# One piece of stacked operands issued earlier, and the order of five engines drawn up anew

## The chip, the cores and the metric

The kernel runs on one core of a Trainium2 chip. The metric is device microseconds (us) for one execution of the whole kernel. The time before is 529.72 us, the median of 3 runs (528.26 to 529.98). All durations below come from one profiled execution of the kernel before.

## The reference, cut to what matters

For each of 8 batches of 512 rows and 256 columns: layer norm, attention over 16 heads of 16 columns, layer norm and residual; then layer norm, a gated feed-forward layer, layer norm and residual.

```python
# x: (8, 512, 256); 16 heads of 16; weights are the same for all batches
x_proj = (layernorm(x) @ w_in.T + b_in).reshape(b, l, 16, -1)
q, k, v = split(x_proj, 3, axis=-1)
att = softmax(einsum('blhd,bmhd->blmh', q, k) * 0.25, axis=2)     # over m
opt = einsum('blmh,blhd->blhd', att, v)        # v of row l times the SUM of its softmax
x = x + layernorm(opt.reshape(b, l, 256) @ w_out.T + b_out)
top1 = argmax(softmax(layernorm(x) @ gate_W.T + gate_b))          # one of 8 experts
inter = relu(layernorm(x) @ wi_W.T + wi_b + lora_of(top1))        # 1024 columns
x = x + layernorm(inter @ wo_W.T + wo_b)
```

Because the attention sum runs over `m` while `v` is taken at `l`, the output of attention is `v` times a sum of softmax values that is 1 but for rounding. The kernel computes the sum from all scores all the same.

## The kernel before, in words

**Units.** A batch has 64 score units: 16 heads times 4 blocks of 128 query rows. For unit `i` TensorE (PE) makes one 128x512 matmul, the score (L227), VectorE (DVE) takes the negated maximum of each row (L692), and ScalarE (ACT) takes the exponential with its row sum (L505). The scores live in a ring of five PSUM banks `ps`, so the score of unit `i` waits until the exponential of unit `i-5` is done. Three more banks, `pu`, serve all other matmuls; a matmul group that takes a `pu` bank waits for the copy that empties it.

**Three engines, one order each.** The order of work on every engine is written out by hand as a table of calls. `slot(s)` in batch `b` is the score of unit `s+4` on PE, the maximum of unit `s+2` on DVE, and the exponential of unit `s` on ACT. Between the slots of batch `b` stand the parts of three neighbouring batches: the norm transposes `x_t(b+1)`, the projections `q_k(b+1, m)` and `value(b+1, t)` of the next batch; the attention output `o_t(b-1)`, `project(b-1)`, the gate and the first feed-forward matmuls `f1(b-1)` of the batch before; and `f2(b-2)` with its norm. Batches 2 to 6 run the same loop body. In batches 0 and 1 there is less of this work, and PE is filled with matmuls of ones that compute nothing (L206), one ahead of each score whose slot is not in the list `FULL`.

**From q_k to the scores.** A projection of 128 rows is evicted twice: ACT writes the rounded high part to `qk` (L519), DVE the low part (L706, semaphore `qk_low`). Then DMAs gather heads from `qk` into `stack`, the operand of the scores. A batch's heads come in four pieces, `stacks(b, 0)` to `stacks(b, 3)`, each 16 units, each 8 DMAs (L1141) issued by the sync engine's queue (SP). `stacks(b+1, 0)` waits for the last of the four low parts of batch `b+1`. `stack` holds three pieces in a ring. And `q_k(b+1, 0)` on ACT overwrites `qk`, so it first waits until the pieces of batch `b` have landed. I number pieces through all batches: batch 0 has pieces 0 to 3, batch 1 begins with piece 4.

**SP's order at the start.** Pieces 1 and 2, and between them `wi`, `lora`, `wib` (late inputs); then a wait for GpSimd (POOL) to have split `wo`, the inputs `x` of batches 2 and 3, which land where `wo` was staged, then piece 3.

**From the last exponential to the next steps.** When a batch's 64 sums are there, DVE computes `ratio` (L790) and `ratio_whole` (L795, `sone`), POOL scales `v` by it (`scale`, L1005), PE transposes it (`o_t`, L239), ACT copies it (L533), and PE projects it (`project`, L285).

Of the kernel before, what the change touches and what calls it, by code (L numbers as in the profile page):

```python
# [21 lines left out]
IDLE, FULL = (25, 6, 4), (8, 28, 32, 35, 39, 50, 53, 61, 69, 71, 73, 75, 76, 82, 84, 90, 96, 98, 99, 100, 102, 103,  # L22
                           105, 107, 109, 112, 115, 117, 121, 126)
# [3 lines left out]
ALL, HALVES = (0, 1, 2, 3), ((0, 1), (2, 3))  # L27
# [6 lines left out]
def sandwich(nc, x, wqk, wv, bqk, wout, wgate, wi, lora, wib, wo, bfree, bg, ident, out):  # L34
    with ExitStack() as ctx:
# [144 lines left out]
        def tensor(e):  # L180
# [270 lines left out]
            slot(0), slot(1), slot(2), slot(3), slot(4), o_t(b - 1, 0), o_t(b - 1, 1), slot(5), slot(6)  # L451
            project(b - 1, 0), slot(7), slot(8), project(b - 1, 1), slot(9), slot(10), x_t(b + 1, 0), slot(11)
            project(b - 1, 2), project(b - 1, 3), x_t(b + 1, 1), slot(12), slot(13), slot(14), slot(15), slot(16)
            slot(17), q_k(b + 1, 0), slot(18), slot(19), q_k(b + 1, 2), slot(20), slot(21), slot(22), slot(23)
            slot(24), slot(25), q_k(b + 1, 1), slot(26), slot(27), slot(28), slot(29), slot(30), slot(31)
            y_t(b - 1, 0), slot(32), slot(33), y_t(b - 1, 1), slot(34), value(b + 1, 0), slot(35), gate(b - 1)
            slot(36), slot(37), gate_t(b - 1), slot(38), q_k(b + 1, 3), value(b + 1, 1), slot(39), slot(40)
            value(b + 1, 2), slot(41), slot(42), value(b + 1, 3), slot(43), slot(44), masked_t(b - 1), slot(45)
            slot(46), slot(47), f1(b - 1, 0), slot(48), slot(49), slot(50), f1(b - 1, 1), slot(51), slot(52)
            f1(b - 1, 2), slot(53), slot(54), slot(55), slot(56), f1(b - 1, 3), slot(57), slot(58), slot(59)  # L460
            slot(60), slot(61), f1(b - 1, 4), slot(62), slot(63), f1(b - 1, 5), f1(b - 1, 6)

            for b in range(2, B - 1):
                slot(0), slot(1), slot(2), f1(b - 2, 7), slot(3), slot(4), o_t(b - 1, 0), o_t(b - 1, 1), slot(5)
                slot(6), slot(7), project(b - 1, 0), slot(8), slot(9), project(b - 1, 1), slot(10), slot(11)
                project(b - 1, 2), project(b - 1, 3), slot(12), slot(13), slot(14), slot(15), f2(b - 2, 0, 0)
                slot(16), f2(b - 2, 0, 1), slot(17), slot(18), f2(b - 2, 1, 0), slot(19), slot(20), f2(b - 2, 1, 1)
                slot(21), slot(22), x_t(b + 1, 0), slot(23), x_t(b + 1, 1), slot(24), slot(25), f2(b - 2, 2, 0)
                slot(26), slot(27), f2(b - 2, 2, 1), slot(28), slot(29), slot(30), f2(b - 2, 3, 0), slot(31)
                slot(32), f2(b - 2, 3, 1), y_t(b - 1, 0), y_t(b - 1, 1), slot(33), slot(34), q_k(b + 1, 0), slot(35)  # L470
                slot(36), gate(b - 1), slot(37), q_k(b + 1, 2), slot(38), slot(39), gate_t(b - 1), slot(40)
                value(b + 1, 0), slot(41), value(b + 1, 1), slot(42), value(b + 1, 2), slot(43), q_k(b + 1, 1)
                slot(44), slot(45), slot(46), value(b + 1, 3), q_k(b + 1, 3), slot(47), slot(48), slot(49)
                masked_t(b - 1), slot(50), f1(b - 1, 0), slot(51), f1(b - 1, 1), slot(52), slot(53), f1(b - 1, 2)
                slot(54), slot(55), slot(56), f1(b - 1, 3), slot(57), slot(58), slot(59), slot(60), f1(b - 1, 4)
                slot(61), slot(62), f1(b - 1, 5), slot(63), f1(b - 1, 6)
            b = B - 1
            slot(0), slot(1), slot(2), f1(b - 2, 7), slot(3), o_t(b - 1, 0), o_t(b - 1, 1), slot(4), slot(5)
            slot(6), project(b - 1, 0), project(b - 1, 1), slot(7), slot(8), slot(9), project(b - 1, 2), slot(10)
            project(b - 1, 3), slot(11), slot(12), f2(b - 2, 0, 0), slot(13), f2(b - 2, 0, 1), slot(14), slot(15)  # L480
            slot(16), slot(17), f2(b - 2, 1, 0), slot(18), slot(19), slot(20), f2(b - 2, 1, 1), slot(21)
            f2(b - 2, 2, 0), slot(22), slot(23), slot(24), slot(25), f2(b - 2, 2, 1), slot(26), slot(27)
            y_t(b - 1, 0), slot(28), y_t(b - 1, 1), slot(29), slot(30), f2(b - 2, 3, 0), gate(b - 1), slot(31)
            slot(32), slot(33), gate_t(b - 1), f2(b - 2, 3, 1), slot(34), o_half(0), slot(35), slot(36), slot(37)
            project(b, 0), slot(38), masked_t(b - 1), slot(39), project(b, 1), slot(40), slot(41), f1(b - 1, 0)
            slot(42), slot(43), slot(44), f1(b - 1, 1), slot(45), f1(b - 1, 2), slot(46), slot(47), slot(48)
            slot(49), f1(b - 1, 3), slot(50), slot(51), slot(52), f1(b - 1, 4), slot(53), slot(54), slot(55)
            f1(b - 1, 5), slot(56), f1(b - 1, 6), slot(57), slot(58), slot(59), f1(b - 1, 7), f2(b - 1, 0, 0)
            more_banks(), f2(b - 1, 0, 1), o_half(1), project(b, 2), project(b, 3), y_half(0), f2(b - 1, 1, 0)
# [6 lines left out]
        def scalar(e):  # L496
# [143 lines left out]
            slot(11), slot(12), slot(13), slot(14), x_t(b + 1, 0), x_t(b + 1, 1), slot(15), slot(16), slot(17)  # L640
            slot(18), slot(19), slot(20), slot(21), slot(22), slot(23), slot(24), slot(25), slot(26), slot(27)
            slot(28), slot(29), slot(30), slot(31), q_k(b + 1, 0), slot(32), slot(33), slot(34), slot(35)
            q_k(b + 1, 2), slot(36), slot(37), slot(38), q_k(b + 1, 1), slot(39), slot(40), slot(41), slot(42)
            slot(43), slot(44), slot(45), slot(46), slot(47), slot(48), slot(49), slot(50), slot(51), q_k(b + 1, 3)
            slot(52), slot(53), slot(54), slot(55), slot(56), slot(57), slot(58), slot(59), slot(60), slot(61)
            slot(62), slot(63), value(b + 1, 0), value(b + 1, 1)
# [610 lines left out]
```

## Time and profile before

| | |
|---|---|
| median of 3 runs | 529.72 us (528.26 to 529.98) |
| the profiled execution, whole | 529.8 us |
| its span, first to last instruction | 528.0 us |
| mean granted TensorE clock | 0.991 |
| PE busy | 504.7 us (96%) |
| DVE busy | 464.7 us (88%) |
| ACT busy | 452.3 us (86%) |
| POOL busy | 345.3 us (65%) |

The chain of work that ended last is 44% PE, 28% ACT, 21% DVE. Three engines are close to full nearly all the time, so the average says little; the stretches in which one of them stands still have to be found one by one. A matmul's busy time contains its passage through the array, so a PE that is 96% busy is not one at its peak.

### The profile page before, as it was taken

To read this page: it belongs to the slowest core of one execution; us is meant where nothing else is said; L and a number is where in the kernel's file an instruction comes from. 1 tells how busy PE (TensorE), PEld (TensorE's weight loads), DVE (VectorE), ACT (ScalarE), POOL (GpSimd) and SP (SyncE) were. 2 spreads that over 40 slices of the span, in tenths; PEclk is the share of its full clock that TensorE was granted. 3 is DMA by queue.
4 is the path that set the end of the run, shared out by engine and by line. 5 is a ranking of instruction groups with operands and counts; after the bars stand their busy time and mean duration, and the time that the engine had idled before them with its cause. 6 is when DMAs were issued, how large, how long until landed. Compare 5 with 4: busy or idle time off the path is not lost.

```text
span 528.0 us, 8930 instructions
## 1 busy us (share of the span) xinstructions
PE 504.7 (96%) x2753; PEld 414.6 (79%) x2753; DVE 464.7 (88%) x1005; ACT 452.3 (86%) x1238; POOL 345.3 (65%) x544
## 2 busy tenths in 40 slices
PE   8999979999999999999999999999999999898995
PEld 6745656678798878888798779887888788677994
DVE  5697969997999999998999899999999899984545
ACT  3598978999989999999999999999999998894330
POOL 5697018512985598729982888559882968696273
PEclk9999979999999999999999999999999999999998
DMA  6685074007240274107430445027400670310002
GB/s 246 187 215 139 1 201 118 2 0 176 64 120 2 52 189 119 41 2 189 111 99 1 118 124 160 1 51 189 120 1 2 172 187 1 81 40 1 1 1 81
DMA packets 22691, 47.63 MB, mean 90 GB/s; under 512 B 5266, under 2 KB 13586, under 8 KB 22004
## 3 DMA queue, kind: packets, MB, share of 16 engines
q1 hardware_dynamic: 21956, 45.95, 32.5%
q0 software_dynamic: 256, 0.52, 0.4%
q10 hardware_dynamic: 432, 0.59, 0.3%
q8 instruction: 22, 0.36, 0.3%
q14 instruction: 25, 0.20, 0.1%
HBM read 8.24 MB, written 4.19 MB: 24 GB/s over the span
## 4 chain that ended last, share of the span: by engine, by line
PE 44%; ACT 28%; DVE 21%; issue 2%; SPq 2%; DMA 1%; POOL 0%; POOLq 0%; ACTq 0%
ACT ps L505 20%; PE pu L199 20%; DVE nmax L692 12%; PE ps L227 9%; PE ps L199 4%; PE pu L285 4%; PE ps L206 3%; DVE st L734 2%; SPq L1141 2%; ACT y L574 2%; ACT qk L519 2%; PE pu L239 1%; ACT inter L568 1%; DMA stack<-qk 1%; DVE mv L739 1%
## 5 line engine op out<-in xcount | busy, mean ns | idle before, releaser
L505 ACT ACTIVATE ps<-ps,nmax 128x512 f32<-128x512 f32 x512 | 346.3, 716 | 13.5 <-DVE nmax L692 12.8
L692 DVE TENSOR_REDUCE nmax<-ps 128x1 f32<-128x512 f32 x512 | 321.2, 679 | 23.4 <-PE ps L227 22.3
L227 PE MATMUL ps<-stack 128*128 128x512 f32 x512 | 182.2, 416 | 1.2 <-DMA stack<-qk 0.7
L505 ACT ACTIVATION_READ_ACCUMULATOR ps<-ps,nmax 128x1 f32 x512 | 134.7, 263 | 0.0
L227 PEld LDWEIGHTS ps<-stack 128*128 128x128 f32 x512 | 93.9, 191 | 20.7 <-ACT ps L505 6.4
L199 PE MATMUL pu<-yT,wi_r 128*128 128x512 f32 x336 | 87.3, 395 | 0.0
L199 PEld LDWEIGHTS pu<-wo_r,inter 128*128 128x128 f32 x648 | 83.8, 188 | 4.2 <-POOL inter L1039 0.7
L199 PE MATMUL pu<-wo_r,inter 128*128 128x256 f32 x648 | 85.6, 282 | 0.5 <-DVE inter L724 0.5
L199 PEld LDWEIGHTS pu<-yT,wi_r 128*128 128x128 f32 x336 | 63.3, 188 | 14.3
L206 PE MATMUL ps<-ones_r 128*128 128x512 f32 x133 | 57.1, 472 | 8.3 <-ACT ps L505 4.0
L206 PEld LDWEIGHTS ps<-ones_r 128*128 128x128 f32 x133 | 27.4, 208 | 33.1 <-ACT ps L505 23.6
L199 PE MATMUL pu<-xnT,wqk_r 128*128 128x512 f32 x192 | 48.9, 393 | 0.7 <-DVE xnT L696 0.7
L982 POOL TENSOR_TENSOR ml<-gs,g 128x128 f32<-128x128 f32 (+1 forms) x9 | 3.5, 389 | 68.6 <-DVE g L844 68.6
L1039 POOL TENSOR_TENSOR inter<-y,inter 128x1024 fp32r<-128x1024 f32 x19 | 45.4, 2391 | 1.5
L199 PEld LDWEIGHTS pu<-xnT,wqk_r 128*128 128x128 f32 x192 | 35.7, 188 | 8.6 <-issue 1.1
L962 POOL TENSOR_TENSOR nmr<-nmr,halves 128x2 f32<-128x2 f32 (+2 forms) x50 | 39.7, 794 | 4.2
L974 POOL TENSOR_TENSOR xb<-xb,y 128x256 f32<-128x256 f32 x58 | 41.1, 736 | 1.8
L1005 POOL TENSOR_TENSOR vo<-vo,sone 128x256 f32<-128x256 f32 x32 | 18.9, 621 | 29.5 <-DVE sone L795 27.8
L285 PE MATMUL pu<-wout_s,oT 128*128 128x256 f32 x128 | 32.2, 384 | 4.3 <-ACT oT L533 3.1
L959 POOL TENSOR_SCALAR nmr<-mv 128x2 f32<-128x2 f32 (+2 forms) x50 | 12.0, 240 | 32.6 <-DVE mv L739 30.8
L968 POOL TENSOR_SCALAR y<-y,nmr 128x256 f32<-128x256 f32 x58 | 31.6, 555 | 2.4
L285 PEld LDWEIGHTS pu<-wout_s,oT 128*128 128x128 f32 x128 | 23.5, 189 | 10.5 <-DVE inter L724 5.7
(154 smaller groups left out, 697.9 us busy)
## 6 DMA issues: line engine op xcount, KB each, us to landing
stack<-qk SPq DMA_DIRECT2D x256, 128.0 KB, 2.5
xb<-in_x SPq DMA_DIRECT2D x7, 512.0 KB, 3.9
out_y<-xb SPq DMA_DIRECT2D x7, 512.0 KB, 3.6
xb<-in_wo SPq DMA_DIRECT2D x1, 1024.0 KB, 5.9
vo<-in_wi SPq DMA_DIRECT2D x2, 512.0 KB, 5.8
oT<-in_wqk ACTq DMA_DIRECT2D x1, 512.0 KB, 4.3
xb<-in_x SPq DMA_DIRECT2D x4, 128.0 KB, 4.2
stack<-qk SPq DMA_DIRECT2D x8, 64.0 KB, 2.5
```

Of the source, the lines that this page charges most:

```text
L199: p = e.matmul(out_, lT(a, c), r(b_, c), start=first and n == 0 and j == 0, stop=last and n == len(chunks) - 1 and j == 2)
L206: e.matmul(bank[:].rearrange("p (k m) -> p k m", k=4), ones_r[:], ones_r[:].unsqueeze(1).to_broadcast([128, 4, 128]), start=True, stop=True)
L227: e.matmul(ps[i % NS][:], st[:, 1 - p, c, t * 128:(t + 1) * 128], st[:, 2, c, :], start=True, stop=True).then_inc(scored, 1)
L285: p = e.matmul(o, oT[:, c, t * 128:(t + 1) * 128], wout_s[:, c, :], start=c == 0, stop=c == 1)
L505: e.activation(ps[i % NS][:], ps[i % NS][:], ACT.Exp, bias=nmax[:, i % 8:i % 8 + 1], accum_out=ssum[:, b % 2, t, h:h + 1]).then_inc(exped, 1)
L692: e.tensor_reduce(nmax[:, i % 8:i % 8 + 1], ps[i % NS][:], AX_X, ALU.max, negate=True).then_inc(maxed, 1)
L959: e.tensor_scalar(nmr[n][:, 0, s], mv[n][:, s, 0], -1.0, None, ALU.mult).then_inc(rstd[i], 1)
L962: e.tensor_tensor(nmr[n][:, 2, s], nmr[n][:, 1, s], halves[:, s], ALU.pow).then_inc(rstd[i], 1)
L968: e.tensor_scalar(dst[:, t, :], src[:, t, :], nmr[n][:, 0, t:t + 1], nmr[n][:, 2, t:t + 1], ALU.add, ALU.mult).then_inc(normed[i], 1)
L974: e.tensor_tensor(xb[:, b % XB, t, :], xb[:, b % XB, t, :], src[:, t, :], ALU.add).then_inc(added[i], 1)
L1005: e.tensor_tensor(vt, vt, sone[:, t, :].unsqueeze(2).to_broadcast([128, H, 16]), ALU.mult).then_inc(scaled, 1)
L1039: e.tensor_tensor(inter[:, 1, f:f + 2, :], whole, high.bitcast(F32), ALU.subtract).then_inc(f1_pool_low, 1)
```

## The change

SP issues piece 3 directly behind piece 2, ahead of its wait for POOL and of `load_x(2)`. `load_x(3)` goes into the loop, behind the last piece of batch 1. The tables of PE, ACT, DVE and the last batch of POOL are new, and so is `FULL`, which has 30 entries as before. No instruction is added or removed; no tile, shape or semaphore value changes.

```diff
-IDLE, FULL = (25, 6, 4), (8, 28, 32, 35, 39, 50, 53, 61, 69, 71, 73, 75, 76, 82, 84, 90, 96, 98, 99, 100, 102, 103,
+IDLE, FULL = (25, 6, 4), (5, 20, 26, 31, 36, 38, 42, 46, 60, 68, 72, 75, 77, 81, 86, 87, 94, 95, 97, 100, 102, 103,
...
@@ PE, b = 0
-            slot(57), slot(58), slot(59), slot(60), value(b + 1, 3), slot(61), slot(62), slot(63)
+            slot(57), slot(58), slot(59), value(b + 1, 3), slot(60), slot(61), slot(62), slot(63)
...
@@ sync
             stacks(0, 2)
+            stacks(0, 3)
             e.wait_ge(late, 12)
-            load_x(2), load_x(3)
-            stacks(0, 3)
+            load_x(2)
             e.wait_ge(late, 21)
...
                 store(b - 3)
-                load_x(b + 2 if b >= 2 else B)
+                if b:
+                    load_x(b + 2)
                 stacks(b + 1, 0), stacks(b + 1, 1), stacks(b + 1, 2)
```

**SP at the start of the program**, from piece 2 on. Three rows of `stack<-qk` are one piece. First before:

```order
L1166 DMA y<-in_wib 2x1024
L1141 DMA stack<-qk 16x2x1024 x2
L1141 DMA stack<-qk 16x2048
L1141 DMA stack<-qk 16x2x1024 x5
L1123 DMA xb<-in_x 128x4x256 x2
L1141 DMA stack<-qk 16x2x1024 x2
L1141 DMA stack<-qk 16x2048
L1141 DMA stack<-qk 16x2x1024 x5
L1172 DMA lb_r<-inter 1x16x64
```

and now (lines in the changed kernel are numbered one higher):

```order
L1167 DMA y<-in_wib 2x1024
L1142 DMA stack<-qk 16x2x1024 x2
L1142 DMA stack<-qk 16x2048
L1142 DMA stack<-qk 16x2x1024 x7
L1142 DMA stack<-qk 16x2048
L1142 DMA stack<-qk 16x2x1024 x5
L1124 DMA xb<-in_x 128x4x256
L1173 DMA lb_r<-inter 1x16x64
```

Pieces 2 and 3 now follow one another, and one load of `x` instead of two stands behind them.

**DVE in batch 0**, from the low parts of `x_t` on: the four `qk` rows are the low parts of batch 1's projections, the last of which lets piece 4 go. Before:

```order
L696 TENSOR_TENSOR xnT<-pu,xnT 128x512 x2
L692 TENSOR_REDUCE nmax<-ps 128x1 x19
L706 SCALAR_TENSOR_TENSOR qk<-pu,bqk_s,qk 128x512
L692 TENSOR_REDUCE nmax<-ps 128x1 x3
L706 SCALAR_TENSOR_TENSOR qk<-pu,bqk_s,qk 128x512
L692 TENSOR_REDUCE nmax<-ps 128x1 x13
L706 SCALAR_TENSOR_TENSOR qk<-pu,bqk_s,qk 128x512
L692 TENSOR_REDUCE nmax<-ps 128x1 x2
L706 SCALAR_TENSOR_TENSOR qk<-pu,bqk_s,qk 128x512
L692 TENSOR_REDUCE nmax<-ps 128x1 x10
L790 RECIPROCAL srec<-ssum 128x64
```

and now:

```order
L696 TENSOR_TENSOR xnT<-pu,xnT 128x512 x2
L692 TENSOR_REDUCE nmax<-ps 128x1 x15
L706 SCALAR_TENSOR_TENSOR qk<-pu,bqk_s,qk 128x512 x2
L692 TENSOR_REDUCE nmax<-ps 128x1 x7
L706 SCALAR_TENSOR_TENSOR qk<-pu,bqk_s,qk 128x512
L692 TENSOR_REDUCE nmax<-ps 128x1 x9
L706 SCALAR_TENSOR_TENSOR qk<-pu,bqk_s,qk 128x512
L692 TENSOR_REDUCE nmax<-ps 128x1 x17
L790 RECIPROCAL srec<-ssum 128x64
```

The last low part stands behind 31 maxima instead of 37, six slots earlier. ACT's high parts of the four stand behind the exponentials of slots 29, 30, 32 and 44 instead of 31, 35, 38 and 51.

**DVE where one repeated batch (2 to 6) passes into the next**, from the last maxima of a batch on: `srec` and `sone` are the sums that the scaling of `v` waits for, `st_0` the norm statistics of the next batch's `x`. Before:

```order
L692 TENSOR_REDUCE nmax<-ps 128x1 x15
L790 RECIPROCAL srec<-ssum 128x64
L734 BN_STATS st_0<-xb 128x6 x4
L739 BN_AGGR mv<-st_0 128x2 x4
L795 TENSOR_TENSOR sone<-ssum,srec 128x64
L692 TENSOR_REDUCE nmax<-ps 128x1 x4
L724 SCALAR_TENSOR_TENSOR inter<-pu,inter 128x512
```

and now:

```order
L692 TENSOR_REDUCE nmax<-ps 128x1 x15
L734 BN_STATS st_0<-xb 128x6 x4
L739 BN_AGGR mv<-st_0 128x2 x4
L692 TENSOR_REDUCE nmax<-ps 128x1
L790 RECIPROCAL srec<-ssum 128x64
L692 TENSOR_REDUCE nmax<-ps 128x1
L795 TENSOR_TENSOR sone<-ssum,srec 128x64
L692 TENSOR_REDUCE nmax<-ps 128x1 x3
L724 SCALAR_TENSOR_TENSOR inter<-pu,inter 128x512
```

The statistics go ahead of both, and two maxima stand ahead of `sone` now. On PE, `o_t` stands behind the score of unit 8 as before, but `f1(b-2, 7)`, which stood three entries ahead of it, is now directly ahead of it.

In the last batch PE now has `o_half(1)`, the transposes of the last scaled half of `v`, between the two parts of `f2(b-1, 0)` instead of behind them; ACT evicts `f1(b-1, 6)` and `f1(b-1, 7)` behind the last exponential instead of ahead of it; DVE takes `ratio_half(1)` ahead of the two low parts of these.

## Rows read from the trace of the kernel before

**Rows 1.** Busy PE, PEld, DVE, ACT, POOL by window; clock, DMA share, GB/s.

```profile
23.10:74.80 51.70, 46.07 (x173) 27.78 (x172) 43.82 (x71) 47.30 (x137) 26.91 (x32) 0.96 0.52 138
74.80:132.90 58.10, 56.15 (x250) 41.55 (x250) 53.53 (x112) 54.45 (x151) 26.37 (x46) 0.97 0.34 85
...
305.40:362.60 57.20, 56.66 (x322) 48.42 (x322) 55.32 (x122) 55.68 (x155) 41.77 (x65) 1.00 0.37 97
```

**Rows 2.** Timeline of ACT: start, us, what, [idle before <- released by].

```profile
43.95 0.86 ACT L505 ACTIVATE ps<-ps,nmax 128x512 f32<-128x512 f32 x1
...
47.52 0.69 ACT L519 ACTIVATE qk<-pu,bqk_s 128x512 fp32r<-128x512 f32 x1 [1.92 <-PE pu L199]
```

**Rows 3.** Timeline of PE: the projection that ACT evicts at 47.52.

```profile
42.88 1.55 PE L199 MATMUL pu<-xnT,wqk_r 128*128 128x512 f32 x6
```

**Rows 4.** Timeline of SP: start, length of the issuing, issues.

```profile
31.04 5.01 SPq L1141 DMA_DIRECT2D stack<-qk  x8
...
38.08 5.55 SPq L1141 DMA_DIRECT2D stack<-qk  x8
...
64.78 25.34 SPq L1141 DMA_DIRECT2D stack<-qk  x31
```

**Rows 5.** Timeline of ACT at the end of batch 0.

```profile
68.35 0.86 ACT L505 ACTIVATE ps<-ps,nmax 128x512 f32<-128x512 f32 x1
...
71.00 0.82 ACT L527 ACTIVATE vo<-pu 128x512 f32<-128x512 f32 x1
74.28 0.60 ACT L527 ACTIVATE vo<-pu 128x512 f32<-128x512 f32 x1 [2.46 <-PE pu L199]
74.77 0.66 ACT L505 ACTIVATE ps<-ps,nmax 128x512 f32<-128x512 f32 x1
...
79.96 1.08 ACT L533 ACTIVATE oT<-pu 128x512 f32<-128x512 f32 x2 [0.34 <-PE pu L239]
```

**Rows 6.** Timeline of PE at the same place.

```profile
71.74 0.80 PE L206 MATMUL ps<-ones_r 128*128 128x512 f32 x1 [2.96 <-DMA stack<-qk]
```

**Rows 7.** Timeline of DVE: the last low part; the first ratio.

```profile
64.01 0.74 DVE L706 SCALAR_TENSOR_TENSOR qk<-pu,bqk_s,qk 128x512 fp32r<-128x512 f32 x1
...
75.32 0.54 DVE L790 RECIPROCAL srec<-ssum 128x64 f32<-128x64 f32 x1
```

**Rows 8.** Busy time by window, columns as in rows 1.

```profile
71.70:78.00 6.30, 6.26 (x18) 5.21 (x19) 3.80 (x7) 3.56 (x11) 1.33 (x3) 0.50 0.83 210
75.30:99.10 23.80, 22.68 (x95) 16.48 (x94) 23.32 (x57) 20.62 (x58) 18.50 (x34) 0.94 0.39 98
```

**Rows 9.** Line L1141, the 8 issues of piece 2.

```profile
DMA to landing us min/median/max: 4.3/4.6/5.1
```

**Rows 10.** Line L1141, the 8 issues of piece 4.

```profile
DMA to landing us min/median/max: 2.4/2.4/2.5
```

**Rows 11.** Timeline of DVE where batch 4 passes into 5.

```profile
305.46 0.54 DVE L790 RECIPROCAL srec<-ssum 128x64 f32<-128x64 f32 x1
305.93 1.34 DVE L734 BATCH_NORM_STATS2 st<-xb 128x6 f32<-128x256 f32 x4
...
307.60 0.19 DVE L795 TENSOR_TENSOR sone<-ssum,srec 128x64 f32<-128x64 f32 x1
307.71 2.47 DVE L692 TENSOR_REDUCE nmax<-ps 128x1 f32<-128x512 f32 x4
```

**Rows 12.** Timeline of POOL, then of PE, at the same place.

```profile
307.93 2.36 POOL L1005 TENSOR_TENSOR vo<-vo,sone 128x256 f32<-128x256 f32 x4 [0.52 <-DVE sone L795]
...
310.59 1.03 PE L239 MATMUL pu<-id_s,vo 128*128 128x128 f32 x8
```

**Rows 13.** Timeline of PE behind the last scores.

```profile
479.59 1.68 PE L199 MATMUL pu<-wo_r,inter 128*128 128x256 f32 x12 [0.48 <-DVE inter L724]
481.49 0.63 PE L356 MATMUL pu<-id_s,vo 128*128 128x128 f32 x4 [0.22 <-POOL vo L1005]
482.90 1.97 PE L285 MATMUL pu<-wout_s,oT 128*128 128x256 f32 x8 [0.78 <-ACT oT L579]
```

More of the change, by code:

```diff
@@ L452, in tensor @@
[L452 to L461, printed above, removed]
+            slot(18), slot(19), q_k(b + 1, 0), slot(20), slot(21), slot(22), slot(23), slot(24), slot(25)
@@ new lines, in tensor @@
+            b = 1
+            slot(0), slot(1), slot(2), slot(3), o_t(b - 1, 0), o_t(b - 1, 1), slot(4), slot(5), slot(6), slot(7)
+            project(b - 1, 0), slot(8), slot(9), slot(10), project(b - 1, 1), slot(11), slot(12), project(b - 1, 2)
+            project(b - 1, 3), slot(13), slot(14), slot(15), slot(16), x_t(b + 1, 0), x_t(b + 1, 1), slot(17)
+            slot(18), slot(19), slot(20), slot(21), q_k(b + 1, 0), slot(22), q_k(b + 1, 2), slot(23), slot(24)
+            slot(25), slot(26), slot(27), slot(28), slot(29), y_t(b - 1, 0), y_t(b - 1, 1), slot(30), q_k(b + 1, 1)
@@ L468, in tensor @@
[L468 to L472, printed above, removed]
@@ L489, in tensor @@
-            more_banks(), f2(b - 1, 0, 1), o_half(1), project(b, 2), project(b, 3), y_half(0), f2(b - 1, 1, 0)
+                slot(16), f2(b - 2, 0, 1), x_t(b + 1, 0), slot(17), slot(18), slot(19), f2(b - 2, 1, 0), slot(20)
+                slot(21), f2(b - 2, 1, 1), slot(22), x_t(b + 1, 1), slot(23), slot(24), slot(25), f2(b - 2, 2, 0)
+                slot(26), f2(b - 2, 2, 1), slot(27), slot(28), slot(29), f2(b - 2, 3, 0), slot(30), f2(b - 2, 3, 1)
+                slot(31), slot(32), y_t(b - 1, 0), y_t(b - 1, 1), slot(33), q_k(b + 1, 0), slot(34), slot(35)
@@ L643, in scalar @@
[L643 to L646, printed above, removed]
+            slot(28), slot(29), q_k(b + 1, 0), slot(30), q_k(b + 1, 2), slot(31), slot(32), q_k(b + 1, 1), slot(33)
@@ L908, in vector @@
-            slot(6), slot(7), slot(8), slot(9), slot(10), project(b - 1, 0), slot(11), y_stats(b - 1, HALVES[0])
-            x_t(b + 1, 0), slot(12), project(b - 1, 1), slot(13), x_t(b + 1, 1), slot(14), y_stats(b - 1, HALVES[1])
-            slot(15), slot(16), slot(17), slot(18), slot(19), slot(20), slot(21), sum_stats(b - 1, HALVES[0])
-            slot(22), slot(23), slot(24), sum_stats(b - 1, HALVES[1]), slot(25), slot(26), slot(27), slot(28)
-            slot(29), slot(30), slot(31), q_k(b + 1, 0), q_k(b + 1, 2), q_k(b + 1, 1), slot(32), slot(33)
@@ new lines, in vector @@
+            slot(6), slot(7), slot(8), slot(9), slot(10), slot(11), slot(12), project(b - 1, 0), slot(13)
+            y_stats(b - 1, HALVES[0]), slot(14), project(b - 1, 1), slot(15), slot(16), y_stats(b - 1, HALVES[1])
+            slot(17), slot(18), slot(19), x_t(b + 1, 0), x_t(b + 1, 1), slot(20), slot(21)
+            sum_stats(b - 1, HALVES[0]), slot(22), slot(23), slot(24), sum_stats(b - 1, HALVES[1]), slot(25)
+            slot(26), slot(27), slot(28), q_k(b + 1, 0), q_k(b + 1, 2), slot(29), slot(30), y_t(b - 1, 0)
@@ L930, in vector @@
-                slot(60), slot(61), slot(62), slot(63)
+                slot(11), project(b - 1, 0), slot(12), y_stats(b - 1, HALVES[0]), slot(13), project(b - 1, 1)
+                slot(14), slot(15), slot(16), slot(17), slot(18), y_stats(b - 1, HALVES[1]), slot(19), slot(20)
+                slot(21), slot(22), sum_stats(b - 1, HALVES[0]), slot(23), slot(24), sum_stats(b - 1, HALVES[1])
+                slot(25), slot(26), slot(27), x_t(b + 1, 0), slot(28), slot(29), slot(30), slot(31), slot(32)
@@ L941, in vector @@
[L941 to L943 removed]
+            slot(5), slot(6), slot(7), slot(8), f1_last(b - 2, 7), slot(9), project(b - 1, 0)
+            y_stats(b - 1, HALVES[0]), slot(10), project(b - 1, 1), slot(11), slot(12), y_stats(b - 1, HALVES[1])
@@ L944, in vector @@
+            slot(42), slot(43), project(b, 0), slot(44), slot(45), y_stats(b, HALVES[0]), slot(46), slot(47)
+            slot(48), slot(49), slot(50), slot(51), slot(52), sum_stats(b, HALVES[0]), slot(53), slot(54), slot(55)
+            slot(56), slot(57), slot(58), slot(59), slot(60), slot(61), ratio_half(1), f1_last(b - 1, 6)
+            f1_last(b - 1, 7), project(b, 1), y_stats(b, HALVES[1]), y_half(0), norm(1, 1, y, y, b, HALVES[1])
             add(1, y, b, HALVES[1]), sum_stats(b, HALVES[1]), gate_half(1, 0), gate_half(2, 0)
```

181 lines of the change are left out of this document (91 added, 90 removed).

## The prediction

> **What bounds the kernel now.** I read the busy time cut at each batch's first exponential first [rows 1]. A repeated batch takes 57.2 us, of which PE is busy 56.7, ACT 55.7 and DVE 55.3. So ACT stands still for 57.2 - 55.7 = 1.5 us in one, and nobody has more to give; a new order can hardly win much there. Batch 0 takes 51.7 us with ACT busy 47.3, and batch 1 takes 58.1 with ACT busy 54.45, although it holds less work than a repeated one. There something waits, and I looked for it in the timelines of that stretch.
>
> ACT stands still twice in batch 0. At 47.52 it has waited 1.92 us to evict `q_k(1, 0)` [rows 2]. The row names PE, but PE's projection ended at 42.88 + 1.55 = 44.4 [rows 3]. The other thing that this eviction waits for is the landing of batch 0's pieces: piece 3 was issued from 38.08 to 43.6 [rows 4], 4 us after ACT could have used it, less its time in flight. The releaser is that DMA.
>
> The second stop is larger. PE has waited 2.96 us at 71.74 for `stack` [rows 6]: piece 4, the first of batch 1, issued from 64.78 on [rows 4], right behind the last low part on DVE, 64.01 + 0.74 = 64.75 [rows 7]. `value(1, 3)` stands on PE behind the score that waits, so ACT has to wait 2.46 us for it [rows 5]. Then PE runs from 71.7 to 78.0 at a granted clock of 0.50, which is the 1.2 GHz level, after having stood still [rows 8].
>
> **The change part by part.** The unit of account is the ACT time of a slot: from 68.35 to 71.00 four exponentials take 2.65 us, 0.66 each [rows 5].
>
> *Piece 3 earlier.* Piece 2's issuing ends at 31.04 + 5.01 = 36.05 [rows 4]; piece 3 follows without the wait and the two loads, and with 5.01 us for it too, it is all issued at 41.1, the last issue at 40.5. How long it flies is the open price. An undisturbed piece lands 2.4 us after issue [rows 10], piece 2, behind `wi` and `lora`, 4.6 [rows 9]. Piece 3 follows piece 2 at the same pace, and the queue is draining; I take 3.8, nearer to piece 2: landing at 44.3. ACT's eviction now stands behind exponential 29 and is due at 43.95, where exponential 30 began [rows 2]. Wait left: 0.4 us instead of 1.9. **-1.5.** Bounds: a landing at 42.9 leaves nothing (-1.9), one at 45.1 leaves 1.2 (-0.7). `load_x(2)` moves to 41 and `load_x(3)` behind the last piece of batch 1, into the middle of that batch. Their first readers are DVE's norm statistics of batch 1, behind the ratio of 75.32 [rows 7], and of batch 2, beyond 120: some 30 us of scores cover each, and without that cover one would cost its flight, 4 to 5 us like that of piece 2.
>
> *Piece 4 earlier.* The last low part moves six maxima up, 6 x 0.66 = 4.0 us, and comes 1.5 earlier by the first term: 64.01 - 5.5 = 58.5. It ends at 59.2, and from there the last part of piece 4 lands after what it took before, 71.7 - 64.8 = 6.9 us, at 66.1. Its score needs the end of exponential 59, where exponential 60 began: 68.35 - 1.5 = 66.85 [rows 5]. The piece is there 0.7 us earlier than it is wanted. That the high part and the projection themselves come in time follows from their places: ACT's stands behind exponential 44, three slots ahead of DVE's turn, PE's behind score 45. `value(1, 3)` stands ahead of score 64 now. So ACT's 2.46 us go, and 0.2 behind them: **-2.7**. If the piece came 1 us late instead, ACT would still be spared its wait for the value, but the maximum would make it wait; I count that as a rival.
>
> *The slow clock.* From 74.77 to 79.96 ACT did six exponentials [rows 5], 5.2 us for 4.0 us of work. With no stop of 3 us there should be no slow stretch: **-1.2**. The cross-check is on DVE, which has 23.3 us of work in 23.8 from 75.3 to 99.1 [rows 8] and so sets the pace of that half of batch 1. Its first ratio waits for exponential 63, which now ends at 71.0 - 1.5 = 69.5, against 75.32 [rows 7]: 5.7 us earlier. My three terms make 5.4. I take **-5.5** for the passage from batch 0 to 1, with bounds -3.5 and -6.5.
>
> The rest of batch 1 contains 3.65 us of ACT idle [rows 1] around `x_t` and the norm statistics. DVE is full there, so I expect none of it back; at most it is 2 us more.
>
> *The repeated batch.* The same work, moved by a slot or two: per group of entries between two waits the sums of PE and ACT work are equal. One place is worse. `sone` began 307.60 - 305.46 = 2.1 us after the last maximum. Now 1.67 us of statistics (305.93 to 307.60), two maxima of 0.6 (four take 2.47) and a ratio of 0.47 stand ahead of it, 3.3 us: 1.2 later [rows 11]. POOL scales in 2.36 and PE's `o_t` began at 310.59 just behind it [rows 12]. `o_t` would begin at 311.5, and `project` waits for its copies, which PE already waits for now. PE, DVE and ACT are all nearly full behind that point, so part of it, 0.3 to 0.5 us, is lost for good. Against it DVE's second `y_stats` comes two slots later, where ACT takes 0.07 us per slot longer than DVE: 0.13 back. **+0.2 in each of five batches, +1.0**, bounds 0 and +0.6 each.
>
> *The end.* PE stands still 0.48 + 0.22 + 0.78 = 1.5 us behind the last scores [rows 13]. The two f1 evictions go behind the last exponential, which so ends 1.1 us earlier; ratio, scaling and `o_half(1)` follow. PE then waits for the scaling ahead of `o_half(1)`, but the copy of it lies under `f2`. About half of the waits go: **-0.7**, bounds 0 and -1.5.
>
> Sum: 529.8 (the profiled execution; its span of 528.0 and 1.8 around it) - 5.5 + 1.0 - 0.7 = 524.6 us. The median of the runs shown, 529.72, is 0.1 below the profiled execution, so it stands for both. A difference of 0.3%, 1.6 us, is about what a measurement of this kernel can tell from no change.
>
> **The rivals.**
>
> *More comes back (chance 0.17).* The idle ACT time around `x_t` in batch 1 is partly there because `x_t` was placed tightly on PE; it now stands six slots later. If 2 us of it go and the repeated batch costs nothing, -5.5 - 2.0 - 0.7 = 521.6. DVE's 98% speak against it.
>
> *Piece 3 flies long (0.10).* If piece 3 cannot overtake what stands ahead in the queues, it lands 4.6 us after issue, at 45.1, and ACT waits 1.2 us: 524.6 + 0.8 = 525.4. The landing of piece 2 speaks for it, that it was already down from 5.1 to 4.3 at its end [rows 9] against. The Trainium skill speaks for this rival (page DMA: Bandwidth & Descriptors, section Queues, rings and completion order): each DMA engine starts the descriptors of one queue in the order of its ring, so piece 3 would still stand behind `lora` and piece 2. The late landing of piece 2 agrees with it, and by it alone the sum would be 525.4, where the landing of an undisturbed piece would make it 524.2.
>
> *The repeated batch costs more (0.12).* If the late `o_t` is lost in full, 0.9 a batch, five times, the sum is -5.5 + 4.5 - 0.7: 528.1, about the edge of no change. For it: three engines above 96% [rows 1]. Against: ACT has 1.5 us of idle time per batch further on that takes up what ACT alone loses.
>
> *The stop at piece 4 stays (0.04).* The low parts come later than I think, or the clock falls for another reason; only piece 3's term and the end remain: 529.8 - 1.5 + 1.0 - 0.7 = 528.6.
>
> *Slower (0.05).* The same place in the repeated batch: `o_t` late by 0.9 and again lost by ACT, whose two copies, then PE's `project`, then DVE's first `project` follow in a row. From (6.2 + 1.6) / 5 = 1.6 us a batch on the kernel is slower by over 0.3%; at 1.8 it takes 529.8 - 6.2 + 9.0 = 532.6. DVE would have to stand still there for over 1 us, which it does nowhere in this stretch now.
>
> **How the numbers follow.** The forecast has 0.52: 522.8 to 526.5 around 524.6. With the rivals below and above, 520.5 to 528.1 holds eight in ten and a little more. Slower has the last rival's 0.05. Same has the stop that stays and some of the costlier repeated batch, 0.08. Faster has the rest, 0.87.
>
> **What the next profile would show.** Right: no ACT wait over 0.5 us at the first `q_k` eviction, no PE wait for `stack` near 67, a granted clock of 1.00 from 66 to 84, the first exponential of batch 1 near 70.6, that of batch 2 near 127.4. Repeated batches of 57.3 to 57.5 with a PE wait for POOL's `vo` ahead of `o_t`. Behind the last exponential some 0.8 us of PE waits. Wrong: a low clock anywhere in batches 0 and 1, or repeated batches off 57.2 by over half a us.

## The result and the profile after

The changed kernel takes 524.18 us, the median of 4 runs, where the kernel before took 529.70 beside it: a ratio of 0.990, with a 95% interval of 0.988 to 0.992. One of the four was a slow run (594.96, mean granted clock 0.774); the other three lie between 523.6 and 524.3. The profiled execution took 524.29, its span 522.5. The forecast was 524.6.

Busy time cut at each batch's first exponential, columns as in [rows 1], changed kernel:

```profile
23.00:70.90 47.90, 45.19 (x177) 27.64 (x175) 44.85 (x73) 46.89 (x136) 26.84 (x32) 1.00 0.56 141
70.90:126.80 55.90, 51.85 (x245) 40.10 (x245) 52.64 (x113) 53.61 (x151) 26.68 (x46) 1.00 0.37 95
...
184.90:242.10 57.20, 56.87 (x322) 47.94 (x321) 55.19 (x121) 55.85 (x156) 41.66 (x65) 1.00 0.35 93
242.10:299.65 57.55, 56.61 (x320) 47.62 (x318) 55.50 (x122) 56.20 (x156) 41.99 (x65) 1.00 0.34 91
299.65:357.30 57.65, 57.30 (x324) 48.49 (x323) 55.07 (x121) 55.88 (x156) 41.50 (x65) 1.00 0.36 94
```

Batch 0 is 3.8 us shorter than in [rows 1] and batch 1 is 2.2 shorter, with the granted clock at 1.00 in both: 6.1 us by the first exponential of batch 2 (126.8 against 132.9). Of these, 1.1 are lost again in batches 4 to 6 (57.6 us each instead of 57.2; batch 3 has its 57.2), and 0.5 come back from there to the end. 6.1 - 1.1 + 0.5 is the 5.5 by which the span fell.

**The first stop.** ACT's timeline at the first `q_k` eviction, the place of [rows 2]:

```profile
43.30 0.75 ACT L505 ACTIVATE ps<-ps,nmax 128x512 f32<-128x512 f32 x1
...
45.16 0.69 ACT L519 ACTIVATE qk<-pu,bqk_s 128x512 fp32r<-128x512 f32 x1 [0.99 <-DMA stack<-qk]
```

SP's timeline, as [rows 4]: pieces 2 and 3 in one row, then the load of `x`, then piece 4 and what follows it.

```profile
30.88 10.11 SPq L1142 DMA_DIRECT2D stack<-qk  x16
41.03 0.72 SPq L1124 DMA_DIRECT2D xb<-in_x  x1
...
59.97 25.98 SPq L1142 DMA_DIRECT2D stack<-qk  x32
```

And the flights of the issues of piece 3 (line L1142, 36 to 41):

```profile
DMA to landing us min/median/max: 3.7/3.9/4.6
```

The wait is 0.99 instead of 1.92 and is now put down to the DMA itself. Piece 3 was all issued at 41.0, and its last issue flew 4.6 us: it landed at 45.0.

**The second stop.** DVE's last low part, then ACT's passage into batch 1, as [rows 7] and [rows 5]; between them two windows, columns as in [rows 8]:

```profile
59.20 0.74 DVE L706 SCALAR_TENSOR_TENSOR qk<-pu,bqk_s,qk 128x512 fp32r<-128x512 f32 x1
```

```profile
66.00:71.00 5.00, 5.00 (x21) 2.81 (x19) 4.75 (x8) 5.00 (x17) 0.00 (x0) 1.00 0.81 203
71.00:78.00 7.00, 5.30 (x25) 3.45 (x25) 6.70 (x18) 7.00 (x22) 4.72 (x9) 1.00 0.65 166
```

```profile
69.30 0.90 ACT L505 ACTIVATE ps<-ps,nmax 128x512 f32<-128x512 f32 x1
...
69.96 1.33 ACT L527 ACTIVATE vo<-pu 128x512 f32<-128x512 f32 x2
70.92 0.92 ACT L505 ACTIVATE ps<-ps,nmax 128x512 f32<-128x512 f32 x1
```

ACT passes through both `vo` evictions without a wait; it is busy for all of the 12 us. The wait for `stack` of [rows 6] is gone: piece 4 landed at 66.9 and PE took its first score at 68.3.

**The repeated batch.** DVE, POOL and PE where batch 3 passes into 4, as [rows 11] and [rows 12]:

```profile
241.09 1.40 DVE L734 BATCH_NORM_STATS2 st<-xb 128x6 f32<-128x256 f32 x4
...
244.39 0.20 DVE L795 TENSOR_TENSOR sone<-ssum,srec 128x64 f32<-128x64 f32 x1
```

```profile
244.74 2.37 POOL L1006 TENSOR_TENSOR vo<-vo,sone 128x256 f32<-128x256 f32 x4 [1.27 <-DVE sone L795]
```

```profile
245.93 1.56 PE L199 MATMUL pu<-yT,wi_r 128*128 128x512 f32 x6
247.32 0.39 PE L330 MATMUL pu<-lt_r,lb_r 98*128 98x512 f32 x1
247.55 1.04 PE L239 MATMUL pu<-id_s,vo 128*128 128x128 f32 x8
```

The batch's first exponential is at 242.1. `sone` comes 2.3 us behind it, where it came 2.2 behind it before (307.60 against 305.4). The statistics began 1.0 us ahead of that exponential; in [rows 11] they began 0.5 behind it. POOL is done at 247.11 and PE reaches `o_t` 0.4 us later, without a wait.

**A stop that is new.** PE's weight loads where batch 4 passes into 5, and the same place in PE's timeline:

```profile
296.76 0.30 PEld L227 LDWEIGHTS ps<-stack 128*128 128x128 f32 x2 [1.03 <-DMA stack<-qk]
```

```profile
296.76 0.72 PE L227 MATMUL ps<-stack 128*128 128x512 f32 x2 [0.59 <-DMA stack<-qk]
```

Piece 20, the first of batch 5, was issued at the usual place behind its low part, but one of its DMAs flew 3.8 us. (PE waits 0.58 us for the first piece of batch 7 too, at 411.94; that stop is not new, the kernel before has it with 0.68 at 417.07.) The flights of that piece, in the changed kernel and then in the kernel before:

```profile
DMA to landing us min/median/max: 2.3/2.5/3.8
```

```profile
DMA to landing us min/median/max: 2.3/2.5/2.6
```

### The profile page after: what moved, and what is told of

The parts are those of the page before. It is cut to its first block, busy times and chain, and to the rows that moved or that the text cites. A ratio compares the mean times of both kernels' runs of the same rounds, so it can differ in the third digit from the quotient of the medians.

```text
span 522.5 us, 8930 instructions
## 1 busy us (share of the span) xinstructions
PE 501.0 (96%) x2753; PEld 411.8 (79%) x2753; DVE 464.2 (89%) x1005; ACT 452.7 (87%) x1238; POOL 344.5 (66%) x544
## 4 chain that ended last, share of the span: by engine, by line
PE 42%; DVE 27%; ACT 17%; SPq 4%; issue 3%; POOL 2%; DMA 2%; POOLq 0%; ACTq 0%
PE pu L199 21%; DVE nmax L692 17%; ACT ps L505 13%; PE ps L227 9%; PE ps L199 4%; SPq L1142 4%; PE pu L285 3%; DVE st L734 3%; DMA stack<-qk 2%; PE pu L330 1%; PE pu L239 1%; PE ps L206 1%; ACT qk L519 1%; DVE y L759 1%; DVE mv L739 1%
## 5 line engine op out<-in xcount | busy, mean ns | idle before, releaser
L227 PE MATMUL ps<-stack 128*128 128x512 f32 x512 | 179.7, 415 | 3.1 <-ACT ps L505 1.7
L206 PE MATMUL ps<-ones_r 128*128 128x512 f32 x133 | 54.8, 454 | 7.6 <-ACT ps L505 6.6
```

Of the source, the lines that this page charges most:

```text
L206: e.matmul(bank[:].rearrange("p (k m) -> p k m", k=4), ones_r[:], ones_r[:].unsqueeze(1).to_broadcast([128, 4, 128]), start=True, stop=True)
L227: e.matmul(ps[i % NS][:], st[:, 1 - p, c, t * 128:(t + 1) * 128], st[:, 2, c, :], start=True, stop=True).then_inc(scored, 1)
```

## The experiments

The changed kernel is made of independent parts: SP's order, and the tables of batch 0, of batch 1, of batches 2 to 6 ("the loop") and of the last batch. The first runs combine them. Ratios are to the kernel before, run beside each; its medians were 529.93 beside the first four, 529.46 beside the next four, 529.25 beside the last four. In the table "to batch 2" is the start of batch 2's first exponential, "loop" the time from there to batch 7's, "end" from there to the last instruction, all in one profiled execution. The intervals are some 1 us to either side, so that two kernels whose medians differ by less are not told apart by their times.

| kernel | median us | ratio (95%) | to batch 2 | loop | end |
|---|---|---|---|---|---|
| before | | 1 | 132.9 | 286.9 | 108.2 |
| changed | 524.18 | 0.990 (0.988 to 0.992) | 126.8 | 288.0 | 107.7 |
| sp_only | 526.81 | 0.995 (0.992 to 0.997) | 129.5 | 287.2 | 108.2 |
| sp_of_before | 528.21 | 0.996 (0.994 to 0.998) | 132.8 | 288.4 | 107.3 |
| loop_of_before | 523.69 | 0.989 (0.986 to 0.991) | 126.7 | 287.2 | 108.0 |
| batch0_new | 524.93 | 0.991 (0.988 to 0.994) | 127.6 | 287.2 | 108.2 |
| last_of_before | 524.32 | 0.992 (0.989 to 0.994) | 126.6 | 287.9 | 107.6 |
| fill_stop | 530.02 | 1.001 (1.000 to 1.003) | 132.5 | 287.7 | 108.2 |
| value_first | 528.16 | 0.998 (0.996 to 0.999) | 131.1 | 286.9 | 108.2 |
| late_low | 526.98 | 0.995 (0.993 to 0.997) | 130.3 | 287.9 | 107.3 |
| sone_early | 524.74 | 0.992 (0.990 to 0.993) | 126.8 | 288.9 | 107.5 |
| f1_7_early | 523.98 | 0.991 (0.989 to 0.992) | 126.4 | 288.2 | 107.5 |
| low_early | 525.65 | 0.994 (0.992 to 0.996) | 126.5 | 289.7 | 107.4 |
| fill_sp | 527.03 | 0.996 (0.995 to 0.997) | 129.1 | 287.4 | 108.2 |

**sp_only**: SP's order alone, over the kernel before.

```diff
             stacks(0, 2)
+            stacks(0, 3)
             e.wait_ge(late, 12)
-            load_x(2), load_x(3)
-            stacks(0, 3)
+            load_x(2)
```

> The kernel before with SP's new order alone (piece 3 behind piece 2, load_x(2) behind it, load_x(3) in the loop); all tables of before. Theory: the wait of ACT at q_k(1, 0) hangs on the landing of piece 3, which is 45.0 in the changed kernel, and the eviction here is due at 45.3, so the 1.9 us wait all but goes and everything behind it, the stop at piece 4 too, moves up as a block: 527.8. Rival: the next stop, for piece 4, takes the time back: 529.7.

3.1 us faster, more than either theory gave. The first stop is gone entirely (piece 3 landed at 44.4), and nothing takes the time back: 2.2 us by slot 32. Another 0.7 lies at the second stop, where ACT waits less, although PE waits as long for `stack`:

```profile
71.14 0.60 ACT L527 ACTIVATE vo<-pu 128x512 f32<-128x512 f32 x1 [1.51 <-PE pu L199]
```

The matmuls of that value run at a granted clock of 0.73 here (69.5 to 72.0), and at 0.50 in the kernel before.

**sp_of_before**: the same edit taken out of the changed kernel.

> The changed kernel with SP's order of before (piece 3 behind the wait and two loads of x). Theory: piece 3 lands near 47.4 again and ACT's eviction of q_k(1, 0), due at 43.95, waits 3.4 us instead of 1.0: 524.2 + 2.4 = 526.6, still without a stop at piece 4. Rival: piece 4 has 1.4 us in hand ahead of its score and takes up part of the delay: 525.2.

4 us slower than the changed kernel by the medians, where I had worked out 2.4. No slack took it up. The profiled execution is the slowest of the 12 (530.31, the median is 528.21), so the length of its wait is not the usual one; ACT's timeline:

```profile
49.82 0.69 ACT L519 ACTIVATE qk<-pu,bqk_s 128x512 fp32r<-128x512 f32 x1 [5.45 <-DMA stack<-qk]
```

Piece 3 landed at 49.7 here, 7.1 us after its issue and behind two loads of `x`, against 5.1 in the profile of the kernel before. PE stood still with it, and the granted clock behind the stop is 0.50 from 52 to 58 us (columns as in [rows 8]):

```profile
54.00:56.00 2.00, 2.00 (x6) 1.27 (x5) 1.47 (x3) 2.00 (x7) 0.00 (x0) 0.50 0.00 0
```

ACT is 4.7 us behind the changed kernel at slot 32 and 6.1 at slot 44, so 1.4 were lost behind the stop. The 12 runs spread from 526.3 to 530.3, those of the changed kernel, without the 594.96, over 0.7 us.

**batch0_new**: SP's order, batch 0's tables and its entries of `FULL`, over the kernel before.

> The kernel before with SP's new order, the tables of batch 0 and the entries of FULL below 64 of the changed one; batches 1 to 7 as before. Theory: the passage from batch 0 to 1 is where the gain comes from, and the tables of batch 1 add little: first exponential of batch 1 at 70.9, of batch 2 at 127.3, time 524.2 to 524.7. Rival: the tables of batch 1 bring the share that came only behind the first exponential of batch 1 (3.9 us were gained there, 6.1 by batch 2): 525.9.

First exponentials at 70.92 and 127.62. Batch 0 with SP's order carries 5.2 of the 6.1 us; the tables of batch 1 bring another 0.8. Cut into groups of four exponentials, batch 1 differs at the transposes: the changed tables are 1.8 us ahead at slots 12 to 16, where here the first `x_t` eviction has waited 0.81 and the second 0.46 and there both still lie ahead, lose this by slot 24, and are ahead again by 0.8 at slots 57 to 60 and at the end of the batch. The waits that the timeline marks for ACT sum to 2.3 us in the changed kernel and 2.5 here, so I can't put the 0.8 down to one of them.

**loop_of_before**: the changed kernel with the loop of before.

> The changed kernel with the tables of before for batches 2 to 6 on PE, ACT and DVE. The step of my prediction (a later sone makes o_t late, 0.2 us a batch) expects 524.2 - 1.0 = 523.2. The theory after the trace: o_t is not late, since PE comes to it 0.4 us after POOL's scaling is done, and the new order costs nothing in itself; what was lost in two of the batches is a late landing of their first piece. Then 524.2, within 0.3.

523.69 against 524.18, and each of the five batches has its 57.2 to 57.3 again (batch 2 its 58.1). The new loop costs 0.9 us in the profile, of which 0.3 come back in the end part. Whether the difference of the two medians is real the intervals don't tell. The batches do point one way: in all seven profiles with the new loop batches 4 and 5 take 57.6 to 58.0, in the five with the old loop and nothing filled in they take 57.2 to 57.3.

**sone_early**: DVE's head of the loop as before, in the changed kernel.

```diff
-                x_stats(b + 1), slot(0), ratio(b - 1), slot(1), ratio_whole(b - 1), slot(2), ...
+                slot(0), ratio(b - 1), x_stats(b + 1), ratio_whole(b - 1), slot(1), slot(2), ...
```

> The changed kernel with DVE's ratio and ratio_whole ahead of the two maxima and of part of the statistics again, as in the kernel before, in batches 2 to 6. The step of my prediction: o_t comes 0.9 us earlier and 0.2 us a batch come back: 523.2. Theory after the trace: PE comes to o_t only behind f1(b-2, 7), 0.4 us after POOL is done, so an earlier sone moves nothing: 524.2, o_t in its old place.

Neither. Its median is 0.6 above the changed kernel's, which the intervals (0.990 to 0.993 and 0.988 to 0.992) don't tell from nothing; but in the profile batch 3 takes 57.5, where it takes 57.2 or 57.3 in the other five that have the new loop and this place of `q_k(b+1, 3)`. DVE's timeline where batch 2 passes into 3 shows a wait of 0.21 for PE ahead of the ratio:

```profile
184.12 0.69 DVE L692 TENSOR_REDUCE nmax<-ps 128x1 f32<-128x512 f32 x1 [0.21 <-PE ps L227]
184.73 0.54 DVE L790 RECIPROCAL srec<-ssum 128x64 f32<-128x64 f32 x1
185.19 1.34 DVE L734 BATCH_NORM_STATS2 st<-xb 128x6 f32<-128x256 f32 x4
```

In the changed kernel the statistics start at 183.81, without a wait, and the next maximum at 185.54. They fill the time in which DVE would stand still for a score. By the profiles, moving them ahead is a small gain, not a loss.

**f1_7_early**: PE's `f1(b-2, 7)` two slots earlier in the loop.

> The changed kernel with PE's f1(b-2, 7) behind slot 2 instead of slot 4 in batches 2 to 6, so that nothing but two scores stands ahead of o_t. Theory: this lays bare what my prediction feared, PE waits 0.9 us for POOL's vo at o_t in each of five batches; the time rises by at most that, 524.2 to 528.7, and I expect 0.3 a batch, 525.7. Rival: PE has that much in hand, 524.2.

523.98, no change, and still no wait for `vo`; `o_t` at 247.15, 0.3 us after POOL was done at 246.82:

```profile
246.70 0.62 PE L227 MATMUL ps<-stack 128*128 128x512 f32 x2
247.15 1.03 PE L239 MATMUL pu<-id_s,vo 128*128 128x128 f32 x8
```

My theory of a cover by `f1(b-2, 7)` fell: PE comes late to `o_t` by all its work ahead of it, in either order of these entries.

**low_early**: `q_k(b+1, 3)` one place earlier on PE, ACT and DVE.

```diff
-                slot(44), value(b + 1, 3), slot(45), q_k(b + 1, 3), slot(46), ...
+                slot(44), q_k(b + 1, 3), slot(45), value(b + 1, 3), slot(46), ...
```

> The changed kernel with q_k(b+1, 3) one place earlier on PE (ahead of value(b+1, 3)), ACT and DVE in batches 2 to 6, so that the first piece of the next batch has 1.5 us in hand instead of 0.9. Theory: a landing that is late by 1.3 us no longer stops PE, and the 0.8 us lost from batch 4 to 5 and the 0.3 from 6 to 7 come back: 523.2. Rival: what was lost there is not owed to the piece: 524.2 or more.

Piece 20 landed 1.7 us ahead of its score and PE did not wait. All batches from 3 on are alike, but alike at 57.8, since the edit costs 0.5 in each at slots 48 to 52. (On ACT it also puts `value(b+1, 1)` two slots later; which of the moves costs the 0.5 was not tried.)

```profile
185.19:242.95 57.76, 57.32 (x322) 48.02 (x321) 55.36 (x122) 56.11 (x156) 41.88 (x65) 1.00 0.35 93
242.95:300.71 57.76, 57.32 (x322) 48.02 (x321) 55.39 (x122) 56.10 (x155) 41.85 (x65) 1.00 0.32 85
```

So the unevenness of batches 3 to 6 is gone together with the late piece, as expected; the 0.8 us did not come back, and as a version it is no good.

**late_low**: DVE's low part of `q_k(1, 3)` behind slot 53 instead of 47.

> The changed kernel with DVE's low part of q_k(1, 3) six slots later (behind slot 53 instead of 47), value(1, 3) still ahead of score 64. Piece 4 would then be issued from 63.9 and land at 70.9, and score 64 start at 71.2 instead of 68.3. Theory: the first exponential of batch 1 comes at 72.4 instead of 70.9, 1.5 us, and a slow clock behind PE's new stop adds about 1.2: 526.9. Rival: with the value out of the way the stop costs its 1.5 us alone: 525.7. Second rival: DVE, full in batch 1, takes it all back: 524.2.

526.98, the first theory's number (526.9). PE's timeline and its clock behind the stop:

```profile
71.69 0.50 PE L227 MATMUL ps<-stack 128*128 128x512 f32 x1 [2.32 <-DMA stack<-qk]
```

```profile
71.70:76.00 4.30, 4.30 (x12) 3.38 (x13) 3.43 (x7) 2.85 (x8) 0.53 (x1) 0.60 0.82 204
```

The first exponential of batch 1 came at 72.95, 2.0 later than in the changed kernel; 0.9 of this is piece 3, which landed 0.9 later in this execution, and 1.1 the stop. By batch 2 it is 3.5: another 1.4 went between slots 0 and 16 of batch 1, behind the stop, where the clock is at 0.60 until 76. Stop and what follows it make 2.6 us, 2.7 in the theory.

**value_first**: the kernel before with `value(1, 3)` ahead of score 64.

> The kernel before with value(1, 3) on PE ahead of the score that waits for piece 4 (between slots 59 and 60), nothing else. Theory: ACT no longer waits 2.5 us for the value, but the piece still lands at 71.7, the score ends at 72.7 and its maximum at 73.7, so the first exponential of batch 1 starts at 73.7 instead of 74.8: 528.6. Rival: my second term was all owed to the place of the value: 527.0.

1.3 us faster. ACT's wait has changed its cause and shrunk by 1.1:

```profile
73.55 0.66 ACT L505 ACTIVATE ps<-ps,nmax 128x512 f32<-128x512 f32 x1 [1.40 <-DVE nmax L692]
```

**fill_stop** and **fill_sp**: 12 matmuls of ones ahead of the wait for piece 4, over the kernel before and over sp_only.

```diff
+                if i == 64:
+                    e.wait_ge(exped, i - NS + 1)
+                    run_idle(ps[i % NS], 12)
```

> The kernel before with 12 more matmuls of ones ahead of PE's wait for piece 4 (about 2.8 us of them at full clock), which compute nothing. The stop for piece 4 stays, but PE doesn't stand still in it. Theory (my third term): the slow clock behind the stop costs 1.2 us and goes: 528.5, with a granted clock of 1.00 between 72 and 78. Rival: the slow clock is hidden behind DVE and ACT: 529.7.

> The kernel before with SP's new order and 12 matmuls of ones, which compute nothing, ahead of PE's wait for piece 4. SP's order alone took 526.8. Theory: the stop for piece 4 stays, the clock stays at 1.00 behind it, and the slow clock's cost of about 1.2 us goes: 525.6. Rival: the filling gives nothing, as over the kernel before: 526.8.

The clock behind the stop is 1.00 in both, but the time didn't fall. Busy time in fill_stop, as in [rows 8]:

```profile
71.70:78.00 6.30, 6.06 (x27) 3.84 (x25) 3.95 (x8) 4.74 (x14) 1.29 (x3) 1.00 0.81 204
```

From exponential 56 of batch 0 to the first of batch 2, fill_stop takes 65.5 us where the kernel before takes 67.2: 1.6 less, and fill_sp 65.7 where sp_only takes 66.2. In fill_stop 1.2 had been lost ahead of that: 0.3 by a later landing of piece 3, and 0.9 behind it, between slots 32 and 42. PE had stood still 1.64 us at this first stop (1.25 in the kernel before, with the clock at 1.00 behind it):

```profile
50.00:52.00 2.00, 2.00 (x6) 1.57 (x7) 1.91 (x3) 2.00 (x6) 0.99 (x2) 0.56 0.00 0
52.00:54.00 2.00, 2.00 (x7) 1.57 (x6) 0.18 (x1) 2.00 (x7) 0.00 (x0) 0.59 0.00 0
```

Another 0.6 (fill_stop) and 0.2 (fill_sp) went in batch 5, whose first piece was late there; the filling also lengthens PE's code, so what lies behind it can shift. So one pair of profiles shows the term with 1.6 us, the other with 0.5, and the times don't show it at all. The run of fill_stop with the highest mean clock (0.999) took 530.57.

**last_of_before**: the changed kernel with the last batch's tables of before.

> The changed kernel with the tables of before for the last batch on PE, ACT, DVE and POOL. My prediction's last term says that the new ones bring 0.7 us: 524.9. The trace gives them 0.5 from the first exponential of the last batch on: 524.7. Rival: nothing, 524.2.

524.32, the rival: no difference that the times tell. In the profile the end takes 107.6 with the old tables and 107.7 with the new behind the new loop, 108.2 and 108.0 behind the old loop.

## Why the prediction was right, step by step

The time lies 0.4 us below the forecast, and the place of the gain, the passage from batch 0 to 1, is as predicted. Of the five terms the first three hold with other sizes: together they had 5.5, and SP's order with batch 0's tables brings 5.2 by batch 2. The last two fell. That the total is off by 0.4 only is in part luck: 0.8 more came in batch 1, where I had nothing, and the +1.1 of the repeated batches has another cause than the one I had priced.

*Piece 3 earlier (-1.5).* Right in mechanism, measured -1.0: landed at 45.0 where I had put 44.3. The rival "piece 3 flies long" is what happened, at 45.1 by its own reckoning. The Trainium skill's rule that I weighed (page DMA: Bandwidth & Descriptors, section Queues, rings and completion order), that descriptors of one queue start in the order of the ring, agrees with this landing to 0.1 us. It isn't proven by it: with the same order on SP the piece landed at 44.4 in the profile of sp_only, which is my figure, and at 45.9 in that of late_low. The piece's flight differs from one execution to the next by more than the two forecasts differ. The weight of the edit is larger than its term: taken out of the new tables it costs 4 us, since those ask for the piece 1.3 us earlier, it flies longer behind two loads of `x`, and time is lost behind the longer stop as well.

*Piece 4 earlier (-2.7) and the slow clock (-1.2).* The low part began at 59.2 (I had 58.5), the piece landed at 66.9 (66.1), the first exponential of batch 1 came at 70.9 (70.6). late_low shows that the six slots carry most of it (2.8 us by the medians), value_first that the place of the value alone is worth 1.3 us and not 2.7. The clock's own share, by the filled stops, is 1.6 us in the profile of the kernel before and 0.5 in that of sp_only. In three more profiles ACT lost time behind a stop, while the clock was at 0.50 to 0.60: 1.4 us in sp_of_before, 1.4 in late_low, 0.9 in fill_stop. There the clock is not separated from the stop itself, and in the times of fill_stop and fill_sp its share does not show, so the size of this term stays open.

*The rest of batch 1 (nothing).* Wrong: its tables brought 0.8 (batch0_new). I had refused it since DVE is 98% busy up to 99.1; up to slot 24 the new tables indeed bring nothing, and the gain shows in the last third of the batch, which I had not looked at. Which wait gives it stays open. Nor was all of the 3.65 us the rest: ACT stands still for 0.7 of them between 74.77 and 79.96, in the slow stretch that the third term had priced already. In the changed kernel ACT stands still for 2.3 us of the batch.

*The repeated batch (+0.2 in each of five).* The sum was nearly right, +1.1 in the profile, by luck, and the reason wrong. The step that failed is "`sone` began 2.1 us after the last maximum. Now ... 3.3 us: 1.2 later": I reckoned from the last maximum as if the statistics would wait for it in the new order too. They start 1.5 us earlier, in DVE's idle time ahead of a late score, and `sone` is 0.1 later. By its profile sone_early is worse without this move. PE never waits for `vo` at `o_t`. Batches 2 and 3 cost nothing; 0.8 is lost in batches 4 and 5, on either side of a late piece, and 0.4 in batch 6, where the next late one is. That the pieces are the cause is not shown: loop_of_before and the kernel before wait 0.5 and 0.7 us for the first piece of batch 7 as well, and their batch 6 takes 57.3 and 57.2.

*The end (-0.7).* Wrong: the new tables of the last batch bring 0 to 0.2. The end part is 0.5 shorter, but with the last batch's tables of before (last_of_before) it is 0.6 shorter, so this comes from what stands ahead of it. The last exponential does start 1.1 us earlier after the batch's first one (57.5 us instead of 58.6), 0.5 of it by the last batch's tables. But PE's three waits of [rows 13], 1.5 us, have become two that sum to 1.4: one for POOL's `vo`, and one further on, at a half's transposes, that was not there before. PE's timeline of the changed kernel:

```profile
475.31 0.63 PE L356 MATMUL ps<-id_s,vo 128*128 128x128 f32 x4 [0.69 <-POOL vo L1006]
...
488.25 0.63 PE L356 MATMUL ps<-id_s,y 128*128 128x128 f32 x4 [0.69 <-DVE y L862]
```

I had costed the waits that are taken away and looked for no new one.

The range and the direction rested on the first three terms, and these carried. Of the signs that I had named, the clock of 1.00 from 66 to 84, PE's passage without a wait near 67 and the first exponentials (70.9 and 126.8 for 70.6 and 127.4) came; an ACT wait under 0.5 us at the first eviction (0.99), a PE wait for `vo` in the repeated batch (none) and only 0.8 us of waits at the end (1.4) did not.

**What stays open.** Whether loop_of_before is really faster than the changed kernel (0.5 us by the medians, 0.7 by the spans), where in batch 1 the 0.8 us come from, and what the slow clock costs in the time.

## What the runs showed of the hardware

Every profile with the new loop but one has a late first piece of batch 5. In six profiles with the new loop (the changed kernel, sp_of_before, late_low, last_of_before, sone_early, f1_7_early) the slowest DMA of piece 20 flew 3.8 to 4.3 us, in low_early 2.6; in the five with the old loop and unlengthened code 2.5 to 2.6 (2.9 and 3.1 in fill_sp and fill_stop, where PE's weight load waited 0.6 and 0.9 for it). The DMA view from that piece's first issue to its landing, in the changed kernel:

```profile
q8 instruction: 1, 0.02, 0.8%
q14 instruction: 1, 0.01, 0.2%
```

and in loop_of_before, where the packet of q8 comes only behind the landing:

```profile
q14 instruction: 1, 0.01, 0.3%
```

One packet on q8, the queue that the profile names "instruction", takes 0.8% of 16 engines' 8.53 us, that is 1.1 us of one engine, and the slowest DMA of the piece lands 1.3 us late. In the changed kernel it starts between 294.0 and 294.5, while the last part of the piece is in flight; in low_early between 295.0 and 295.5, when the piece is about to land (at 295.7) and nothing is late, in loop_of_before at 296, behind the landing at 295.7. That all six late ones have such a packet in the flight is shown; that it is the cause is my reading of it, since no run moved the packet alone, and low_early shows that a packet in the flight does not always delay it. The Trainium skill (page Runtime: NRT & Kernel Launch, section Instruction fetch mechanics) says that an engine's sequencer fetches its code by DMA in blocks of 16 KiB and that the cost is mostly hidden. The size agrees (22 packets on q8 with 0.36 MB are 16 KB each); if my reading is right, it is hidden only where the transfer that it delays has more than 1.3 us in hand. The same piece one batch earlier landed 0.9 us ahead of its score.

The time of one kernel is uneven from run to run, and in part this goes with the clock. The kernel before spread from 528.0 to 534.0 over its runs, and in the 19 runs beside the first four kernels the four slowest (532.4 to 534.0) have the four lowest mean clocks (0.984 to 0.989). At the first stop PE stood still 1.25 us in one profile and its clock stayed at 1.00, 1.64 us in another and it fell to 0.56, near the 1.2 GHz level, and 0.9 us more were lost behind it: a stop that differs by 0.4 us between two executions can make their times differ by more. The stops are not the whole of it. Of the kernels without the stop at piece 4, loop_of_before spread from 523.4 to 523.9 only, but last_of_before from 523.9 to 527.2 and low_early from 524.7 to 528.0.

## What to carry to other kernels

A wait names the engine that was last by the profile; look at where that engine's work really ended, and at what the instruction waits for besides, before pricing it. When work is moved ahead on an engine, reckon its new start from what it needs itself and from that engine's idle time, not from the instruction that used to stand ahead of it. And look at how much a transfer that a full engine waits for has in hand, above all where the same margin comes back in every batch: here one landing that was 1.3 us late used up a margin of 0.9.
